# Attention on one core: where two groups of 32-column matmuls stand in the order of rounds

## The chip, the core and the metric

The kernel runs on one core of a Trainium2 chip. The core has a matrix engine (TensorE, PE in the profile, whose weight loads are shown as PEld), VectorE (DVE), ScalarE (ACT), GpSimd (POOL), SyncE (SP), which here only issues DMAs, and 16 DMA engines. All work in parallel, each in the order of its own program, and wait for each other by semaphores. The metric is the device time of one execution in microseconds (us); less is better.

## The reference, cut to what matters

```python
x = x + attention(layernorm(x), ctx, ctx)   # 8 batches, 512 tokens, 512 wide, 16 heads of 32
#   scores = Q K^T / sqrt(32);  attn = softmax(scores);  out = (attn V) Wo^T + bo
h = layernorm(x)
logits = h @ router_weight.T + router_bias  # 8 experts, the best 2 of each token
x = x + sum over the two chosen experts of weight * expert(h)
```

Everything is float32. The experts' part follows the attention and is untouched here.

## The kernel before, in words

The attention is cut into 32 units: 8 batches times 4 groups (c = 0 to 3) of four heads. A unit is worked on in stages that are spread over several steps; a step s is one turn of the pipeline, and `step(s)` writes down, in 8 rounds, what the engines do in it. `ORDER` is the list of all steps' entries, and every engine runs through that one list and picks out its own, so the order within a round is the order on each engine. In what follows c is the remainder of s by 4.

In step s TensorE works on unit s and on three neighbours:

- `max` (row_max, line 443), once in each round: two matmuls of scores of unit s+1 into the one buffer `max_ps`, from which VectorE takes the rows' maxima (line 674, 1024 columns). The `max` of the next round writes the same buffer, so it waits until that reduction has ended (line 431).
- `exp` (line 455), twice in each round: scores again, which ScalarE takes from a work bank through the exponential into `pt` (line 563).
- `weigh` (line 467), in rounds 1, 3, 5 and 7: four heads of `pt` times V. Each matmul has 32 columns of weights, and the four heads fill four strips of 32 columns. Being float32, each matmul appears twice in the trace, so the group of four is 8 records.
- `sum` (line 475), once in a step: the column of ones times `acc`, the sum of the exponentials that GpSimd adds up (lines 754 and 757). It is four matmuls of 32 columns as well. ScalarE copies the result to `inv` (line 569), and VectorE inverts it and divides (`norm`, lines 685 and 690), one quarter in each of four rounds.
- the projections of unit s+2: `k` (line 402, in two halves of 6), `q` (line 410, two halves of two matmuls, 4 records), `v` (line 424, two times 12). Steps with c = 2 have them in other rounds: both halves of `q` in rounds 0 and 1, `k` in rounds 3 and 4. So in a step with c = 2 round 2 holds no projection.
- for finished tokens: the output projection `out` (line 488, two halves of 4 records, in rounds 6 and 7), the transposition `turn_xln` of the normalised rows (line 373, round 5), the router's columns `logits` (route_logits, line 380: four matmuls of 32 columns, one for each quarter of the width), and `logit_sum` (line 386, round 0), which adds the four quarters up.
- `turn_max` (line 449) opens a step: the maxima of unit s are transposed, split by ScalarE (line 553) and VectorE (line 678) and sent by two DMAs to where `exp` of unit s reads them from round 1 on.

The work banks are four buffers of PSUM for everything but `max`, `weigh` and the first tiles. A small planner gives each use, in the order of the list, the bank that has been out of use longest; TensorE then waits until the bank's use before has been read (`take`). Moving an entry therefore also changes which bank, and so which reader, the entries behind it wait for.

In steps with c = 1 ScalarE also normalises the next batch's input in rounds 1 and 2 (`ln1`, line 538). Step 32 and the rounds after it are the end of the attention: the last divisions, output projections, second normalisations and router's columns, one token tile after another.

The lines touched are 151 and 152 (`sum` in round 2), 163 (`logits` in round 6) and 187 (`norm` in rounds 3 to 6).

Of the kernel before, what the change touches and what calls it, by code (L numbers as in the profile page):

```python
# [54 lines left out]
def attention_stage(nc, x, ctx_t, w_t, bq, bk, bv, bo, router_wt, router_b, out, xln_dram, logits, ident):  # L55
    B, S, D = x.shape
    C = D // P
    T = S // P
# [4 lines left out]
    units, bs = range(B * C), range(B)  # L63

    with ExitStack() as ctx:
# [62 lines left out]
        def step(s):  # L128
# [3 lines left out]
            def at(r, *keys):  # L132
                rounds[r] += keys
# [3 lines left out]
            for r in range(8):  # L137
# [10 lines left out]
                    at(r, ("weigh", s - 1, T - 1))  # L148
                if r % 2 and r > 1 and s in units:
                    at(r, ("weigh", s, (r - 3) // 2))  # L150
            if s - 1 in units:
                at(2, ("sum", s - 1))


            if s - 6 in tokens[:-T]:
# [2 lines left out]
            if s - 5 in tokens[:-T]:  # L158
                at(0, ("x2", s - 5))
                at(1, ("rstd", s - 5))  # L160
                at(4 if c == 2 else 3, ("ln2", s - 5))
                at(5, ("turn_xln", s - 5))
                at(6, ("logits", s - 5))
            if s - 4 in tokens[:-T]:
                at(6, ("out", s - 4, 0))
                at(7, ("out", s - 4, 1))
# [17 lines left out]
                        at((r + t) % 8, *keys)  # L184
            if s - 1 in units[:-1]:
                for t in range(T):
                    at(3 + t, ("norm", s - 1, t))

            if s + 2 in units:
                u = s + 2  # L190
# [60 lines left out]

        tokens = range(B * T)
        ORDER = [key for s in range(-2, B * C + 3) for key in step(s)]


# [61 lines left out]
        at = {key: n for n, key in enumerate(ORDER)}  # L317
# [1345 lines left out]
```

## Time and profile before

| | us |
|---|---|
| three runs | 1777.14, 1781.18, 1782.40 |
| median | 1781.18 |
| the profiled execution | 1776.77 |
| its span | 1775.1 |
| TensorE busy in the span | 1633.1 (92%) |
| VectorE busy | 1242.6 (70%) |
| GpSimd busy | 803.3 (45%) |
| ScalarE busy | 654.2 (37%) |

The attention takes the first 998 us of the span, the choice of experts the next 60, the experts the rest. A timeline row gives the start from the span's begin, the duration, the engine, the line, the tiles and how many records were merged into it; what stands in brackets is the idle time of that engine before the row and who ended it. "issue" there means that no wait of a semaphore explains it. A merged row's duration runs from its first start to its last end.

### The profile page before, as it was taken

The page shows a single profiled execution, that of the slowest core. Times are in us where ns is not written, and L with a number is a line of the kernel's source. Part 1 is how long each engine was busy: PE and PEld are TensorE (multiplying, and loading weights), DVE is VectorE, ACT ScalarE, POOL GpSimd, SP SyncE. Part 2 cuts the span into 40 slices and gives each one's busy share as a digit, 9 for nine tenths or more (in the row PEclk, how much of TensorE's full clock was granted, in tenths as well). Part 3 has the DMA queues.
Part 4 walks back from the last instruction along what each step waited for, and adds up shares of the span by engine and source line. Part 5 has one row for each costly group of instructions (what it writes and reads, how often), then busy time and mean ns, then how long its engine had stood idle before and what let it go on. Part 6 is the DMA issues. An engine that isn't in the chain of part 4 may idle for free. (4 is left out here: it accounts for less than half of the span.)

```text
span 1775.1 us, 30007 instructions
## 1 busy us (share of the span) xinstructions
PE 1633.1 (92%) x9637; PEld 1178.9 (66%) x9637; DVE 1242.6 (70%) x2223; ACT 654.2 (37%) x1265; POOL 803.3 (45%) x619
## 2 busy tenths in 40 slices
PE   4798999999999999999997349999999999999996
PEld 3454555555555555555543149999999998999995
DVE  3566667776776777666673668777888778867874
ACT  3253444544445445344442123223333224222321
POOL 3255556555556565555665122333434333343422
PEclk9899999999999999999999559999999999999998
DMA  5332333343433434333321251334443245233422
GB/s 190 96 106 70 98 111 95 95 115 86 124 91 101 109 78 126 86 96 95 95 72 36 69 184 44 90 92 160 147 164 122 89 141 185 94 97 132 126 71 73
DMA packets 98804, 188.69 MB, mean 106 GB/s; under 512 B 26320, under 2 KB 27344, under 8 KB 98640
## 3 DMA queue, kind: packets, MB, share of 16 engines
q1 hardware_dynamic: 79408, 123.99, 24.7%
q0 software_dynamic: 19232, 62.73, 11.1%
q8 instruction: 77, 1.26, 0.3%
q14 instruction: 87, 0.71, 0.1%
HBM read 204.19 MB, written 37.36 MB: 136 GB/s over the span
## 5 line engine op out<-in xcount | busy, mean ns | idle before, releaser
L674 DVE TENSOR_REDUCE negmax<-max_ps 128x2 f32<-128x1024 f32 x256 | 312.4, 1220 | 207.6 <-PE max_ps L443 207.2
L563 ACT ACTIVATE pt<-work 128x512 f32<-128x512 f32 x512 | 278.7, 595 | 274.6 <-PE work L455 261.5
L757 POOL TENSOR_TENSOR acc<-acc,pt 128x1024 f32<-128x1024 f32 x128 | 303.4, 2372 | 134.6 <-ACT pt L563 133.8
L1292 PE MATMUL gu_ps<-xgT_hi,wg_hi 128*128 128x256 f32 x1248 | 355.1, 285 | 0.0
L1292 PE MATMUL gu_ps<-xgT_hi,wg_lo 128*128 128x256 f32 x1248 | 352.0, 282 | 0.0
L1292 PE MATMUL gu_ps<-xgT_lo,wg_hi 128*128 128x256 f32 x1248 | 351.6, 282 | 0.0
L754 POOL TENSOR_TENSOR acc<-pt 128x1024 f32<-128x1024 f32 x64 | 155.6, 2432 | 264.2 <-ACT pt L563 264.2
L1292 PEld LDWEIGHTS gu_ps<-xgT_hi,wg_hi 128*128 128x128 f32 x1248 | 235.7, 189 | 0.0
L1292 PEld LDWEIGHTS gu_ps<-xgT_lo,wg_hi 128*128 128x128 f32 x1248 | 235.7, 189 | 0.0
L1292 PEld LDWEIGHTS gu_ps<-xgT_hi,wg_lo 128*128 128x128 f32 x1248 | 235.5, 189 | 0.0
L443 PE MATMUL max_ps<-ks,qs 96*128 96x512 f32 x512 | 200.6, 473 | 24.3 <-DMA qs<-q_lo 15.4
L1531 POOL DMA_INDIRECT out<-acc,idx x78 | 77.3, 991 | 321.3 <-DVE acc L1440 321.3
L1352 ACT ACTIVATE sig<-gate 128x256 f32<-128x256 f32 x156 | 65.1, 418 | 328.9 <-DVE gate L1404 328.9
L455 PE MATMUL work<-qs,ks 98*128 98x512 f32 x512 | 168.0, 405 | 7.3 <-DMA qs<-m_lo 5.8
L443 PEld LDWEIGHTS max_ps<-ks,qs 96*128 96x128 f32 x512 | 89.5, 193 | 86.7 <-issue 65.0
L467 PE MATMUL o_ps<-pt,v 128*32 128x512 f32 x1024 | 136.4, 605 | 1.3 <-ACT pt L563 1.3
L410 PE MATMUL work<-xT,wq 128*128 128x512 f32 x256 | 126.2, 616 | 5.1 <-ACT pt L563 5.1
L1305 PE MATMUL d_ps<-wd_hi,hid_hi 128*128 128x512 f32 x312 | 124.2, 398 | 5.0 <-DVE acc L1437 5.0
L1526 POOL DMA_INDIRECT acc<-out,idx x78 | 80.5, 1031 | 101.1 <-DMA out<-acc,idx 88.7
L488 PE MATMUL work<-wo,oT 128*128 128x512 f32 x240 | 120.6, 626 | 5.9 <-DVE oT L690 3.4
L455 PEld LDWEIGHTS work<-qs,ks 98*128 98x128 f32 x512 | 95.8, 190 | 43.8 <-issue 12.1
L685 DVE RECIPROCAL inv<-inv 128x128 f32<-128x128 f32 x128 | 120.7, 943 | 4.6 <-ACT inv L569 4.6
(199 smaller groups left out, 2824.6 us busy)
## 6 DMA issues: line engine op xcount, KB each, us to landing
raw_g<-w_gate_up SPq DMA_DIRECT2D x39, 2048.0 KB
raw_d<-w_down SPq DMA_DIRECT2D x39, 1024.0 KB
ks<-k_hi SPq DMA_DIRECT2D x252, 64.0 KB, 2.0
qs<-q_hi SPq DMA_DIRECT2D x252, 64.0 KB, 2.0
bd<-b_down SPq DMA_DIRECT2D x39, 256.0 KB
x_in<-x SPq DMA_DIRECT2D x32, 256.0 KB, 3.1
ctxT_raw<-ctx_t SPq DMA_DIRECT2D x32, 256.0 KB, 4.0
x<-x SPq DMA_DIRECT2D x32, 256.0 KB, 2.9
```

The lines of the kernel that those rows point to most:

```text
L410: ins = e.matmul(to[:, :], wq[:, k, cols], xT[:, k, :], start=(k == 0), stop=(k == C - 1))
L443: ins = e.matmul(max_ps[:, j, :], qs[i][0:3 * HD, h, t * P:(t + 1) * P], ks[i][0:3 * HD, h, :], start=True, stop=True)
L455: e.matmul(to[:, :], ks[i][0:3 * HD + 2, h, k * P:(k + 1) * P], qs[i][0:3 * HD + 2, h, :], start=True, stop=True).then_inc(exp_ready.sem, 1)
L467: ins = e.matmul(o_ps[u % 2][HD * h:HD * (h + 1), :], v[:, k, c * P + HD * h:c * P + HD * (h + 1)], pt[k % 2][:, h, :], start=(k == 0), st ...
L488: ins = e.matmul(to[:, :], oT[b % 2][:, k, t * P:(t + 1) * P], wo[:, k, :], start=(k == 0), stop=(k == C - 1))
L563: e.activation(pt[k % 2][:, h, :], in_work("exp", u, k, h)[:, :], ACT.Exp, scale=scale).then_inc(exped.sem, 1)
L674: e.tensor_reduce(negmax[:, u % 2, n:n + 2], max_ps[:, :, :], AX.X, ALU.max, negate=True).then_inc(maxed.sem, 1)
L685: e.reciprocal(inv[:, cols], inv[:, cols]).then_inc(inverted.sem, 1)
L754: e.tensor_tensor(acc[:, heads, :], pt[0][:, heads, :], pt[1][:, heads, :], ALU.add).then_inc(added.sem, 1)
L757: e.tensor_tensor(acc[:, heads, :], acc[:, heads, :], pt[k % 2][:, heads, :], ALU.add).then_inc(added.sem, 1)
L1292: ins = e.matmul(gu_ps[n % GU_BANKS][:, part, :], wg[s][pw][:, k, cols], xgT[s][px][:, k, :], start=(k == 0 and m == 0), stop=(k == KD - 1 ...
L1305: ins = e.matmul(d_ps[j][:, :], hid[s][px][:, k, j * P:(j + 1) * P], wd[s][pw][:, k, :], start=(k == 0 and m == 0), stop=(k == KF - 1 and ...
```

## The change

`sum` of unit s-1 stands in round 3 instead of round 2, behind that round's `weigh` (in step 32, which has no such `weigh`, it stays in round 2). `logits` of token tile s-5 stands in round 7 instead of round 6, behind that round's `weigh`. The four divisions of a unit stand in rounds 4 to 7 instead of 3 to 6. No instruction is added or removed. The lines behind the change are 2 higher in the changed kernel.

```diff
@@ step(s) @@
                 if r % 2 and r > 1 and s in units:
                     at(r, ("weigh", s, (r - 3) // 2))
-            if s - 1 in units:
-                at(2, ("sum", s - 1))
+
+                if r == (2 if s == B * C else 3) and s - 1 in units:
+                    at(r, ("sum", s - 1))
+                if r == 7 and s - 5 in tokens[:-T]:
+                    at(r, ("logits", s - 5))
...
                 at(5, ("turn_xln", s - 5))
-                at(6, ("logits", s - 5))
...
             if s - 1 in units[:-1]:
                 for t in range(T):
-                    at(3 + t, ("norm", s - 1, t))
+                    at(4 + t, ("norm", s - 1, t))
```

TensorE in step 17 (c = 1), from round 2 to the beginning of round 4; the numbers behind `work` are the banks. Before:

```order
L443 MATMUL max_ps<-ks0,qs0 128x512 x2
L455 MATMUL work1<-qs2,ks2 128x512
L455 MATMUL work3<-qs2,ks2 128x512
L475 MATMUL work2<-acc,ones 32x512 x4
L410 MATMUL work1<-xT,wq 128x512 x2
L443 MATMUL max_ps<-ks0,qs0 128x512 x2
L455 MATMUL work3<-qs2,ks2 128x512
L455 MATMUL work2<-qs2,ks2 128x512
L467 MATMUL o_ps1<-pt0,v 32x512 x4
L410 MATMUL work1<-xT,wq 128x512 x2
L443 MATMUL max_ps<-ks0,qs0 128x512 x2
```

and with the change:

```order
L445 MATMUL max_ps<-ks0,qs0 128x512 x2
L457 MATMUL work1<-qs2,ks2 128x512
L457 MATMUL work3<-qs2,ks2 128x512
L412 MATMUL work0<-xT,wq 128x512 x2
L445 MATMUL max_ps<-ks0,qs0 128x512 x2
L457 MATMUL work1<-qs2,ks2 128x512
L457 MATMUL work3<-qs2,ks2 128x512
L469 MATMUL o_ps1<-pt0,v 32x512 x4
L477 MATMUL work2<-acc,ones 32x512 x4
L412 MATMUL work0<-xT,wq 128x512 x2
L445 MATMUL max_ps<-ks0,qs0 128x512 x2
```

The ones product has moved behind the weighing, and the query projection has bank 0 instead of bank 1, which the first of the two `exp` just ahead of it fills.

TensorE in step 14 (c = 2), rounds 2 and 3. Before:

```order
L443 MATMUL max_ps<-ks0,qs0 128x512 x2
L455 MATMUL work3<-qs2,ks2 128x512
L455 MATMUL work2<-qs2,ks2 128x512
L475 MATMUL work0<-acc,ones 32x512 x4
L443 MATMUL max_ps<-ks0,qs0 128x512 x2
L455 MATMUL work3<-qs2,ks2 128x512
L455 MATMUL work2<-qs2,ks2 128x512
L467 MATMUL o_ps0<-pt0,v 32x512 x4
```

and with the change:

```order
L445 MATMUL max_ps<-ks0,qs0 128x512 x2
L457 MATMUL work1<-qs2,ks2 128x512
L457 MATMUL work0<-qs2,ks2 128x512
L445 MATMUL max_ps<-ks0,qs0 128x512 x2
L457 MATMUL work2<-qs2,ks2 128x512
L457 MATMUL work1<-qs2,ks2 128x512
L469 MATMUL o_ps0<-pt0,v 32x512 x4
L477 MATMUL work0<-acc,ones 32x512 x4
```

Between the `max` of round 2 and that of round 3 only the two `exp` are left.

TensorE in step 11 (c = 3), rounds 6 and 7. Before:

```order
L443 MATMUL max_ps<-ks,qs 128x512 x2
L455 MATMUL work<-qs,ks 128x512 x2
L380 MATMUL work<-xlnT,rw_cols 32x128 x4
L488 MATMUL work<-wo,oT 128x512 x2
L443 MATMUL max_ps<-ks,qs 128x512 x2
L455 MATMUL work<-qs,ks 128x512 x2
L467 MATMUL o_ps<-pt,v 32x512 x4
L488 MATMUL work<-wo,oT 128x512 x2
```

and with the change:

```order
L445 MATMUL max_ps<-ks,qs 128x512 x2
L457 MATMUL work<-qs,ks 128x512 x2
L490 MATMUL work<-wo,oT 128x512 x2
L445 MATMUL max_ps<-ks,qs 128x512 x2
L457 MATMUL work<-qs,ks 128x512 x2
L469 MATMUL o_ps<-pt,v 32x512 x4
L382 MATMUL work<-xlnT,rw_cols 32x128 x4
L490 MATMUL work<-wo,oT 128x512 x2
```

The router's columns now follow the weighing of round 7.

## Rows read from the trace of the kernel before

**Rows 1.** The page: its head, and a row of section 5 (count | busy, mean ns).
```profile
span 1775.1 us, 30007 instructions
...
L685 DVE RECIPROCAL inv<-inv 128x128 f32<-128x128 f32 x128 | 120.7, 943 | 4.6 <-ACT inv L569 4.6
```

**Rows 2.** Windows: busy us of PE, PEld, DVE, ACT, POOL; PEclk, DMA share, GB/s.
```profile
200.00:900.00 700.00, 685.14 (x3475) 381.24 (x3468) 486.60 (x699) 325.06 (x608) 399.62 (x229) 1.00 0.38 100
```

**Rows 3.** Timeline, step 11, rounds 2 to 3: start, us, engine, what [idle before <-releaser].
```profile
376.41 0.63 PE L443 MATMUL max_ps<-ks,qs 96*128 96x512 f32 x2
...
376.88 0.63 PE L455 MATMUL work<-qs,ks 98*128 98x512 f32 x2
...
377.44 1.07 PE L475 MATMUL work<-acc,ones 128*32 128x512 f32 x8
...
378.97 0.19 PEld L410 LDWEIGHTS work<-xT,wq 128*128 128x128 f32 x1 [0.24 <-issue]
379.40 0.19 PEld L410 LDWEIGHTS work<-xT,wq 128*128 128x128 f32 x1 [0.24 <-issue]
...
380.73 0.63 PE L455 MATMUL work<-qs,ks 98*128 98x512 f32 x2
```

**Rows 4.** Timeline, step 11, round 4, which holds no 32-column group.
```profile
384.57 0.63 PE L455 MATMUL work<-qs,ks 98*128 98x512 f32 x2
...
385.16 0.29 PE L424 MATMUL work<-wv_lo,ctxT_hi 128*128 128x256 f32 x1
385.29 0.28 PE L424 MATMUL work<-wv_hi,ctxT_lo 128*128 128x256 f32 x1
...
386.95 0.63 PE L455 MATMUL work<-qs,ks 98*128 98x512 f32 x2
```

**Rows 5.** Timeline, step 11, round 6, with the router's columns.
```profile
390.90 0.63 PE L455 MATMUL work<-qs,ks 98*128 98x512 f32 x2
391.46 0.43 PE L380 MATMUL work<-xlnT,rw_cols 128*32 128x128 f32 x8
...
394.27 0.63 PE L455 MATMUL work<-qs,ks 98*128 98x512 f32 x2
```

**Rows 6.** Timeline, step 14, round 2 and the start of round 3.
```profile
464.33 0.63 PE L455 MATMUL work<-qs,ks 98*128 98x512 f32 x2
464.53 1.22 DVE L674 TENSOR_REDUCE negmax<-max_ps 128x2 f32<-128x1024 f32 x1 [0.29 <-PE max_ps L443]
...
465.89 0.30 PEld L443 LDWEIGHTS max_ps<-ks,qs 96*128 96x128 f32 x2 [0.84 <-DVE negmax L674]
...
466.46 0.84 PE L455 MATMUL work<-qs,ks 98*128 98x512 f32 x2
```

**Rows 7.** Timeline, step 30, round 3 and the start of round 4.
```profile
923.08 1.22 DVE L674 TENSOR_REDUCE negmax<-max_ps 128x2 f32<-128x1024 f32 x1 [0.92 <-PE max_ps L443]
...
924.44 0.30 PEld L443 LDWEIGHTS max_ps<-ks,qs 96*128 96x128 f32 x2 [0.84 <-DVE negmax L674]
```

**Rows 8.** Timeline, step 17, rounds 2 and 3.
```profile
547.78 0.63 PE L455 MATMUL work<-qs,ks 98*128 98x512 f32 x2
...
549.50 1.07 ACT L563 ACTIVATE pt<-work 128x512 f32<-128x512 f32 x2
...
550.13 1.98 PE L410 MATMUL work<-xT,wq 128*128 128x512 f32 x4 [0.73 <-ACT pt L563]
...
552.43 0.63 PE L455 MATMUL work<-qs,ks 98*128 98x512 f32 x2
```

**Rows 9.** Timeline, VectorE at the start of step 15.
```profile
485.24 0.28 DVE L678 TENSOR_TENSOR m_lo<-work,m_hi 16x128 fp32r<-16x128 f32 x1 [1.63 <-ACT m_hi L553]
```

**Rows 10.** Timeline, step 32, end of the attention: router's columns and their copies.
```profile
987.47 0.66 PE L380 MATMUL work<-xlnT,rw_cols 128*32 128x128 f32 x8
...
989.67 0.59 ACT L575 ACTIVATE xlnT<-work 128x512 f32<-128x512 f32 x1
...
991.13 0.28 ACT L581 ACTIVATE parts<-work 128x128 f32<-128x128 f32 x1 [0.88 <-PE work L380]
```

## The prediction

> **What bounds the kernel now.** I began with the page's head [rows 1]: the span is 1775.1 us, and the execution it belongs to took 1776.77. The change touches the attention alone, so the next view was busy time by windows: over 700 us of steady attention TensorE is busy 685.14, VectorE 486.60, GpSimd 399.62, ScalarE 325.06, at full granted clock (1.00 of 2.4 GHz) [rows 2]. There TensorE sets the end, and the question is what TensorE loses between its instructions and where it waits. A busy row can't tell that, since the matmuls' ends are modelled; start-to-start distances can. So I read TensorE's timeline round by round, from the first `exp` of a round to the first `exp` of the next.
>
> A round without a 32-column group shows what full-width work costs: from 384.57 to 386.95 are 2.38 us [rows 4]. Two `exp` and two `max` take 0.47 a pair (376.41 to 376.88 [rows 3]), and 12 `v` matmuls 0.12 each (385.16, 385.29 [rows 4]): 0.94 + 1.44 = 2.38, with nothing lost.
>
> A round with `sum` and half a `q` goes from 376.88 to 380.73, 3.85 us [rows 3]. The `q` half is 4 records at 0.43 (378.97, 379.40 [rows 3]), 1.71; with 0.94 that is 2.65. The `sum` group therefore costs 3.85 - 2.65 = 1.20. Its 8 records run as two waves of four: together 1.07 us, where one takes 0.6, so the second wave starts 0.45 behind the first. Two waves are 0.85 (at 0.43, the pace of a 512-column record) to 0.91 us of streaming, and about 0.32 are lost in going from 128 columns to 32 and back. The round with `logits` and half an `out` goes from 390.90 to 394.27, 3.37 us [rows 5]: the group costs 3.37 - 2.65 = 0.72, though two waves of 128 columns stream for only about 0.25.
>
> The Trainium skill's page "TensorEngine Tiling (Array Packing)", section "Key Properties", says that changing the tiling mode drains TensorE and that changing only the tile does not. The trace agrees as far as it goes: the four heads of one group start without a gap, and each lone group loses about 0.32. Two groups side by side stand nowhere in the trace; by that page the second would cost its streaming alone.
>
> **The change, term by term.** The same instructions run; what changes is neighbours and waits.
>
> 1. `sum` in steps with c = 0, 1 or 3 (steps 1 to 29: 22 of them). In round 2 it costs 1.20 and goes. Behind the weighing of round 3 it adds two waves. Bounds: 0.85 if only streaming is added, 1.20 if every group pays for itself. I take 0.88, the middle of the streaming bounds, because heads within a group change without loss. Gain 0.32 x 22 = 7.0 us. What comes late next in round 2 would be VectorE's reduction, but a round of 2.65 leaves it its 2.13 (term 3).
>
> 2. The bank of `q` in steps with c = 1. There the same round takes 547.78 to 552.43, 4.65 us, 0.80 more than in step 11, and the first `q` waits for ScalarE's exponential, which is late because the normalisation of the input runs ahead of it [rows 8]. With the change `q` takes another bank, long read, and the wait has no cause. The next that needs those exponentials is the `exp` pair of round 3, 2.65 later than 547.78, at 550.4. The wait of `q` ended at 550.13, when the first bank was read; the second is read one exponential on (two take 1.07, so 0.5), 550.6, and the second `exp` wants it at about 550.7. So bounds are 0 and 0.80; I take all 0.80, for 7 steps (1, 5, ... 25; step 29 has no next batch): 5.6 us gain.
>
> 3. `sum` in steps with c = 2 (2, 6, ... 30: 8 steps). Here round 2 is not TensorE's: the reduction starts at 464.53, and the load for the next `max` goes at 465.89, 1.36 later, with VectorE as releaser [rows 6]. In step 30 it is 923.08 and 924.44, again 1.36 [rows 7]. The round takes 464.33 to 466.46, 2.13 us, and `sum` lies inside it for nothing: `max` and `exp` pairs with 1.20 are 2.14, just the time of the reduction's loop. Without `sum` the round stays at 2.13 with TensorE idle in its place, and round 3 grows by 0.88. Loss 8 x 0.88 = 7.0. In step 30 the divisions delay the reduction of round 4 a little, which the shift mends by 0.1 to 0.2; I count 6.9. Bounds: 0 gained in round 2 and 1.20 lost in round 3 at one end, 0.32 gained as in term 1 at the other.
>
> 4. `logits`, 27 token tiles (steps 5 to 31). Round 6 loses 0.72. Behind the weighing two short waves add 0.25 of streaming; but the way back to full width is longer behind a short group: it costs 0.72 against 1.20, 0.48 less, where 0.64 of streaming (8 records of 384 fewer columns in two waves, 0.32 each) is missing, so 0.16 stay. Bounds 0.25 and 0.72; I take 0.40. Gain 0.32 x 27 = 8.6 us.
>
> 5. The divisions one round later. Nothing on TensorE waits for them within three rounds. VectorE's round 7 gets 0.94 for the reciprocal [rows 1], about 0.3 for the product. Behind it stands `m_lo`, for which two DMAs and then `exp` of round 1 wait. Before it VectorE is idle for 1.63 at the fullest place, the end of a step with c = 2 [rows 9]; 1.3 fit, and the step's turn comes 0.4 later by the moved `logits`. Cost 0; if the cover were gone, what sticks out of some 30 steps. ScalarE's copy of the sums and GpSimd's first addition, which waits for `sum`, have a round of slack: 0.
>
> 6. The end. `logits` of tile 27 moves in step 32 from before the transposition of tile 28 to after the last `out`. Before, `logits` of tile 28 started at 987.47 right behind that `out` [rows 10]. Now tile 27 stands there; ScalarE copies tile 28's rows only after it, since both use one buffer; then tile 28 follows. One copy ends at 990.26 and the next one that needs a `logits` after it starts at 991.13 [rows 10], so the way from copy to `logits` and on to a copy is 0.87; with the copy's own 0.59 the detour is 1.46. From there to the end the chain is PE, ACT, PE for each tile, so nothing takes it back. Loss 1.5, bounds 0 and 2. In step 31, where ScalarE sets the pace, the moved `sum` counts 0, between a gain of 0.3 and a loss of 1.2.
>
> Sum: -7.0 - 5.6 + 6.9 - 8.6 + 1.5 = -12.8 us. The profiled execution would take 1764.0. It was 4.4 below the median of 1781.18; I put the change on the median: 1768.4.
>
> **Rivals.**
>
> A. Every group pays for itself, side by side or not (a drain by group, or by the bank it writes). Then terms 1 and 4 are 0, term 3 is 8 x 1.20 less 0.1 = +9.5, and with -5.6 and +1.5 it is 5.4 slower: 1786.6. For it: no pair is in the trace. Against: four heads in four strips follow each other without a gap. By the Trainium skill's rule on tiling modes it would be wrong. It decides when a second group costs over 1.10: at that price terms 1, 3 and 4 (0.10 x 22 gained, 8.7 lost, logits near 0.10 x 27) just eat the rest.
>
> B. VectorE's wait is no loss in steps with c = 2 (as if `sum` had not hidden it): -12.8 - 6.9 - 2.6 = -22, 1759. Two places with the same 1.36 speak against it.
>
> C. The wait of term 2 comes back at round 3, on `exp` or on the weighing: -7.2, 1774. For it: ScalarE is behind by two normalisations. Against: the margin above, thin as it is.
>
> D. `m_lo` comes late through the division in round 7, and `exp` of round 1 waits for its DMA in all steps: 0.4 in each would eat the gain (31 x 0.4 = 12.4), and 0.6 makes it 6 slower, 1787. Against it the idle 1.63.
>
> **How the numbers follow.** Forecast 0.66, A 0.07, B 0.05, C 0.14, D 0.05, something else (the places of the low-clock stretches at start and end) 0.03. The likeliest one's own range is 1763 to 1773: terms 1, 3 and 4 move together with the price of the second group, 0.03 on some 57 groups, 1.7 us; the exit behind `logits` is worth up to 4 to the fast side; the three runs spread by 5.3. With B and C inside, the range is 1759 to 1776. A measurement tells about 0.3%, 5.3 us, from no change. Faster by more holds for the forecast, B and most of C, 0.80; same 0.12; slower 0.08 (A, D).
>
> **What would show it.** In the changed profile: the timeline of step 11 has rounds 2 and 6 at 2.65 and round 3 at 3.84 + 0.88; the round of step 14 stays at 2.13 with the load for `max` still released by VectorE and TensorE idle some 0.9 before it, which is new; step 17 shows no wait on ScalarE at `q`; PE's idle before `m_lo`'s readers is as before. Steps with c = 0 and 3 shorten by 0.64, with c = 1 by 1.44, and those with c = 2 grow by 0.56. If the distance from the weighing's start to that of the ones product is over 0.91, my price is wrong; if round 2 of step 14 gets shorter than 2.13, term 3 is.

## The result, and the profile after

| | before | after |
|---|---|---|
| median, us (lowest to highest) | 1781.18 (1777.14 to 1782.40) | 1761.12 (1759.76 to 1763.00) |
| ratio, with its 95% interval | | 0.9894 (0.9881 to 0.9906) |
| profiled execution, us | 1776.77 | 1761.72 |
| its span | 1775.06 | 1760.01 |

The changed kernel is 1.06% faster by the ratio, 18.9 us at the median before (the medians are 20.1 apart). The forecast was 1768.4 in a range of 1759 to 1776. The profiled pair differs by 15.05 us, against a sum of 12.8; before's profiled execution was 4.4 below its median, after's 0.6 above.

Where sum and traces differ is read from the distances between one `turn_max` and the next, step by step. Us saved by the steps of each kind, as the sum said and as the two traces have it:

| steps | predicted | measured |
|---|---|---|
| c = 0 (4 to 28) | 4.2 | 4.9 |
| c = 1 (1 to 29) | 10.4 | 11.0 |
| c = 2 (2 to 30) | -4.7 | -3.1 |
| c = 3 (3 to 27) | 4.2 | 5.6 |
| step 31 and the end of the attention | -1.2 | -3.0 |
| everything else | 0 | -0.4 |

First the lines of the page and of the windows that answer to [rows 1, 2], with the same columns: count | busy, mean ns | idle; and busy us of PE, PEld, DVE, ACT, POOL, then clock, DMA share, GB/s.

```profile
span 1760.0 us, 30007 instructions
...
L687 DVE RECIPROCAL inv<-inv 128x128 f32<-128x128 f32 x128 | 120.6, 942 | 8.9 <-ACT inv L571 8.9
```

```profile
200.00:900.00 700.00, 684.43 (x3557) 398.37 (x3557) 504.91 (x720) 335.45 (x621) 411.28 (x236) 1.00 0.39 102
```

The same 700 us now hold 82 more matmul records (3557 against 3475, 2.4%), while TensorE's busy time is the same. Steps 8 to 29 together are 2.6% shorter (616.3 us against 632.5). The gain does not show as less idle time, but as more work in the same busy time.

Step 11, rounds 2 to 4, answers to [rows 3]; start, us, engine, what:

```profile
372.86 0.63 PE L457 MATMUL work<-qs,ks 98*128 98x512 f32 x2
...
375.51 0.63 PE L457 MATMUL work<-qs,ks 98*128 98x512 f32 x2
...
376.07 1.06 PE L469 MATMUL o_ps<-pt,v 128*32 128x512 f32 x8
376.95 1.04 PE L477 MATMUL work<-acc,ones 128*32 128x512 f32 x8
...
380.22 0.63 PE L457 MATMUL work<-qs,ks 98*128 98x512 f32 x2
```

Round 2 takes 375.51 - 372.86 = 2.65, round 3 takes 4.71. Round 3 was 3.85, so the ones product behind the weighing costs 0.86, where alone it cost 1.20. From the weighing's start to its own are 0.88.

Rounds 6 and 7 of the same step, to [rows 5]:

```profile
386.54 0.63 PE L457 MATMUL work<-qs,ks 98*128 98x512 f32 x2
...
389.19 0.63 PE L457 MATMUL work<-qs,ks 98*128 98x512 f32 x2
...
389.75 1.07 PE L469 MATMUL o_ps<-pt,v 128*32 128x512 f32 x8
...
390.63 0.40 PE L382 MATMUL work<-xlnT,rw_cols 128*32 128x128 f32 x8
...
390.96 1.98 PE L490 MATMUL work<-wo,oT 128*128 128x512 f32 x4
...
392.78 0.27 PE L451 MATMUL work<-ident,negmax 128*16 128x128 f32 x1
```

Round 6 is 2.65 (it was 3.37). Round 7, up to the next `turn_max`, is 3.60 (it was 3.38): 0.72 go and 0.22 come. From the first record of the router's columns to the `out` behind them are 0.33: two short waves and nothing more.

Step 14, round 2, to [rows 6]:

```profile
457.07 0.63 PE L457 MATMUL work<-qs,ks 98*128 98x512 f32 x2
457.27 1.23 DVE L676 TENSOR_REDUCE negmax<-max_ps 128x2 f32<-128x1024 f32 x1 [0.28 <-PE max_ps L445]
...
458.55 0.30 PEld L445 LDWEIGHTS max_ps<-ks,qs 96*128 96x128 f32 x2 [1.28 <-DVE negmax L676]
458.55 0.73 PE L445 MATMUL max_ps<-ks,qs 96*128 96x512 f32 x2 [0.85 <-DVE negmax L676]
459.12 0.63 PE L457 MATMUL work<-qs,ks 98*128 98x512 f32 x2
```

As forecast, the load still waits for VectorE and TensorE now idles 0.85 where the ones product stood. The round takes 2.05 instead of 2.13: with the ones product gone the load follows the reduction's start by 1.28 instead of 1.36.

Another wait has gone, in round 3. In before the second `exp` of round 3 waited for ScalarE to read the bank:

```profile
466.81 0.19 PEld L455 LDWEIGHTS work<-qs,ks 98*128 98x128 f32 x1 [0.30 <-ACT pt L563]
```

That pair of `exp` took 0.84 from 466.46 on [rows 6]; the same pair in after takes 0.63 from 459.12 on and shows no wait. The banks have changed (see the order of step 14 above): before, round 3 took banks 3 and 2, which the `exp` pair of round 2 had just filled; now it takes 2 and 1.

Step 17, to [rows 8]: the query projection starts 0.47 behind the first `exp` of its round and shows no wait.

```profile
539.58 0.63 PE L457 MATMUL work<-qs,ks 98*128 98x512 f32 x2
...
540.05 1.88 PE L412 MATMUL work<-xT,wq 128*128 128x512 f32 x4
...
542.24 0.63 PE L457 MATMUL work<-qs,ks 98*128 98x512 f32 x2
```

VectorE at the start of step 15, to [rows 9]: the idle time before `m_lo` has fallen from 1.63 to 0.59, and `m_lo` still starts 0.61 behind `turn_max`.

```profile
477.43 0.27 PE L451 MATMUL work<-ident,negmax 128*16 128x128 f32 x1
...
478.04 0.28 DVE L680 TENSOR_TENSOR m_lo<-work,m_hi 16x128 fp32r<-16x128 f32 x1 [0.59 <-ACT m_hi L555]
```

The end, to [rows 10]. Tile 27's router's columns stand at 970.40 and tile 28's wait for the copy between them:

```profile
970.40 0.65 PE L382 MATMUL work<-xlnT,rw_cols 128*32 128x128 f32 x8
971.18 0.60 ACT L577 ACTIVATE xlnT<-work 128x512 f32<-128x512 f32 x1 [8.35 <-PE work L382]
...
971.92 0.66 PE L382 MATMUL work<-xlnT,rw_cols 128*32 128x128 f32 x8 [0.87 <-ACT xlnT L577]
```

One thing that the forecast lacks stands in step 31. Three windows of after, then the one of before at the same place in the program (columns as in [rows 2]):

```profile
895.00:921.00 26.00, 20.74 (x103) 9.68 (x101) 18.62 (x28) 11.73 (x23) 18.59 (x11) 1.00 0.09 31
921.00:928.00 7.00, 6.26 (x22) 2.32 (x26) 1.49 (x1) 3.15 (x6) 3.24 (x4) 0.52 0.21 78
928.00:955.00 27.00, 23.59 (x101) 9.63 (x94) 9.16 (x15) 7.27 (x14) 15.92 (x9) 1.00 0.09 29
```

```profile
941.00:948.00 7.00, 6.52 (x41) 1.91 (x37) 4.91 (x7) 4.77 (x10) 4.50 (x4) 1.00 0.11 40
```

In after's profile the granted clock was 0.52 for 7 us, the lower level of 1.2 GHz, and from the `turn_max` of step 31 to the ones product of step 32 it took 33.38 us against 31.39. Both kernels have the same idle time at its start, here in after's timeline and then in before's:

```profile
921.74 1.19 PE L457 MATMUL work<-qs,ks 98*128 98x512 f32 x2 [2.15 <-DMA qs<-m_lo]
```

```profile
940.23 0.70 PE L455 MATMUL work<-qs,ks 98*128 98x512 f32 x2 [2.15 <-DMA qs<-m_lo]
```

Eleven of the twelve experiments told below show a fall there as well, for 3.4 or 6.8 us, `e4_norm_only` among them, which runs TensorE in the order of before; `e10_low_early` and before show none. Nothing ties the fall to the change. `e10_low_early` runs TensorE in step 31 in after's order, and without a fall it takes 31.09 for the stretch that took 33.38. By that comparison the fall cost 2.3 in after. This stretch is 2.0 of the 3.0 us lost there; the other 1.0 is the tail, from there to the attention's end (30.21 against 29.24).

### The profile page after: what moved, and what is told of

It reads as the page before. It is cut to its first block and busy times, and to the rows that moved or that the text cites. A ratio compares the mean times of both kernels' runs of the same rounds, so it can differ in the third digit from the quotient of the medians.

```text
span 1760.0 us, 30007 instructions
## 1 busy us (share of the span) xinstructions
PE 1615.5 (92%) x9637; PEld 1187.8 (67%) x9637; DVE 1247.7 (71%) x2223; ACT 658.1 (37%) x1265; POOL 800.0 (45%) x619
## 5 line engine op out<-in xcount | busy, mean ns | idle before, releaser
L1307 PE MATMUL d_ps<-wd_lo,hid_hi 128*128 128x512 f32 x312 | 123.6, 396 | 0.0
```

The source lines that it names most:

```text
L1307: ins = e.matmul(d_ps[j][:, :], hid[s][px][:, k, j * P:(j + 1) * P], wd[s][pw][:, k, :], start=(k == 0 and m == 0), stop=(k == KF - 1 and ...
```

## The experiments

Each was timed against runs of the kernel before on the same chip, and the ratio is to those; so two experiments are best compared by their ratios. The lengths of rounds are from the first `exp` of one to that of the next. Means of steps with c = 3 are over steps 11 to 27, those of steps with c = 2 over steps 10 to 26.

**The ones product alone.** The kernel of after with the router's columns back in round 6.

```diff
-                if r == 7 and s - 5 in tokens[:-T]:
-                    at(r, ("logits", s - 5))
...
                 at(5, ("turn_xln", s - 5))
+                at(6, ("logits", s - 5))
```

> Only the ones product moves behind the weighing (round 3) and the divisions one round later; the router's columns stay in round 6. If a second 32-column group pays its streaming alone (0.86 us behind a weighing against 1.20 alone, as the changed kernel's rounds show), 22 steps with c = 0, 1, 3 give 0.34 each (7.5), the wait of the query projection in 7 steps with c = 1 goes (0.65 net each, 4.6), and 8 steps with c = 2 lose 0.56 each (4.5): 7.6 us faster than before, about 1773.5. Rival, all of the gain comes from the sum and its banks: near the changed kernel's 1761. Rival, the sum gives nothing because the steps with c = 2 eat it: within 2 us of before.

1774.17 us, ratio 0.9964 (0.9950 to 0.9978): 6.4 us gained.

**The router's columns alone.** The kernel of before with only `logits` moved to round 7.

> Only the router's columns move behind the weighing of round 7; ones product and divisions as before. Round 6 loses 0.73 and round 7 gains 0.22 in 27 steps: 13.8 us faster, less about 1 for the detour at the attention's end: 12.8 faster than before, about 1768. By the price of the prediction (0.40 behind the weighing, 1.5 at the end) it would be 7.1 faster, 1774.

1774.06 us, ratio 0.9961 (0.9944 to 0.9977): 6.9 us gained, where each of the 27 columns saves 0.50 in its own two rounds, 13.5 in all. Half is missing. Steps with c = 2 did shorten, from a mean of 28.20 to 27.65, but steps with c = 3 grew from 28.25 to 29.17. There the distance from `turn_max` to the first `exp` was 1.3 to 2.5 us in five of six steps (7 to 27), where it is 0.57 when nothing waits, and in steps 15 and 19 the granted clock fell to 0.50 for 3.4 us right behind it. The last runs look for what this wait is.

**The divisions alone.** The kernel of before with `norm` in rounds 4 to 7.

> Only the divisions one round later. Theory: VectorE had the room, 0 within 1 us. Rival, part of the gain comes from reductions of the maxima that start earlier in rounds 4 to 7: 2 to 4 us faster. Rival, the reduced idle time before m_lo costs: slower by 0.3 in each of 31 steps, 9 us.

1780.71 us, ratio 1.0003 (0.9992 to 1.0014): no cost in the time. The trace shows where one is hidden. In steps with c = 1, here 17, `max` behind round 1 now waits for VectorE's reduction, which starts 1.99 behind the first `exp` of the round (0.89 in before):

```profile
546.86 1.21 DVE L674 TENSOR_REDUCE negmax<-max_ps 128x2 f32<-128x1024 f32 x1
...
548.13 0.30 PEld L443 LDWEIGHTS max_ps<-ks,qs 96*128 96x128 f32 x2 [0.46 <-DVE negmax L674]
```

Round 1 of these steps (5 to 25) takes 3.82 to 3.86 instead of 3.54 to 3.59, and round 2, where `q` waits for ScalarE, is shorter by as much (4.32 to 4.38 instead of 4.65).

**Not side by side.** The kernel of after, but the ones product ahead of the two `exp` of round 3, so that it and the weighing are each alone.

```diff
+                if r == (2 if s == B * C else 3) and s - 1 in units:
+                    at(r, ("sum", s - 1))
                 u, j = (s, r - 1) if r else (s - 1, 7)
                 if u in units:
                     at(r, *[("exp", u, j // 2, 2 * (j % 2) + i) for i in range(2)])
```

> The changed kernel with the ones product in the same round 3, but ahead of the two exp instead of right behind the weighing, so that it stands alone among 128-column work; the router's columns still behind the weighing. If neighbourhood is what saves, each of 30 steps loses 0.34 against the changed kernel: 10 us slower than it, about 1771. If what saves is only the other round or the other banks, it is equal to the changed kernel, 1761.

```profile
379.34 1.03 PE L445 MATMUL max_ps<-ks,qs 96*128 96x512 f32 x2
380.30 1.07 PE L477 MATMUL work<-acc,ones 128*32 128x512 f32 x8
381.29 0.73 PE L457 MATMUL work<-qs,ks 98*128 98x512 f32 x2
381.96 1.07 PE L469 MATMUL o_ps<-pt,v 128*32 128x512 f32 x8
```

1771.07 us, ratio 0.9951 (0.9936 to 0.9966). In steps with c = 0 rounds 2 and 3 together take 3.74 + 3.95 = 7.69 us, against 2.65 + 4.71 = 7.36 in after. The same work in the same step costs 0.33 more when the neighbour is full width. That is the price of going to 32 columns and back, measured by itself. Over the 30 steps moved it is 10 us, as expected.

**The bank of `q`.** The kernel of after with one rule in the planner, which gives `q` in steps with c = 1 the bank that the `exp` ahead of it fills, as in before.

```diff
+                if kind == "q" and what[0] % C == 3 and 3 <= what[0] < B * C - C:
+                    bank = free.index(at["exp", what[0] - 2, 0, 2])
```

> The changed kernel, but in the 7 steps with c = 1 in which ScalarE also normalises the next input, the query projection is given the bank of the first exp of round 2 again, as in the kernel before. Theory: round 2 of these steps goes from 2.65 back to about 3.45, with TensorE waiting for ScalarE: 4.6 to 5.6 us slower than the changed kernel, about 1766. Rival, the wait went because the ones product no longer stands between: no difference.

Step 17, round 2 (start, us, what, idle before):

```profile
551.97 0.63 PE L459 MATMUL work<-qs,ks 98*128 98x512 f32 x2
...
554.17 3.15 PE L414 MATMUL work<-xT,wq 128*128 128x512 f32 x4 [1.57 <-ACT pt L567]
```

1778.92 us, ratio 0.9994 (0.9977 to 1.0011): nearly all of the change's gain is gone. The expectation was 1766, and its price for the wait was wrong. Round 2 took 4.45 to 4.49 in four of the seven steps against 2.65, so the wait is 1.84 and not 0.80. In the other three (1, 5 and 17) it took 6.01 to 6.34, because behind the wait the granted clock fell to 0.50 for 3.4 us. In before the bank came free 2.35 us behind the first `exp` of the round [rows 8], and 1.20 of the ones product lay inside that wait; only what stuck out of it, 0.80, showed. The mechanism holds, and it is worth more than its term said: had the planner not given `q` another bank, moving the ones product would have made these steps longer. Round 2 would be 0.2 shorter than in before, and round 3 0.86 longer.

**Steps with c = 2 left as they were.** The kernel of after with the ones product of these steps in round 2.

```diff
-                if r == (2 if s == B * C else 3) and s - 1 in units:
+                if r == (2 if s == B * C or c == 2 else 3) and s - 1 in units:
```

> The changed kernel, but in the steps with c = 2 (2, 6, ... 30) the ones product stays in round 2, where TensorE waits for the reduction anyway. Theory: these 8 steps lose no 0.56 (0.88 by the prediction) any more: 4.5 to 7 us faster than the changed kernel, 1754 to 1757; and if the low-clock stretch in step 31 of the changed kernel comes from the emptier rounds of step 30, about 2 more. Rival, the reduction's wait in round 2 is no free place: equal to the changed kernel or slower.

1758.87 us, ratio 0.9871 (0.9849 to 0.9893), against 1754 to 1757 expected; after's interval overlaps with it, so a gain isn't shown. Rounds 2 and 3 went from 2.05 + 4.37 to 2.13 + 3.73, 0.56 shorter in steps 2 to 26. But again the steps behind them, with c = 3, grew: a mean of 28.20 against 27.51. Part of it is one fall of the clock, to 0.50 for 3.4 us in step 15.

**A shorter reduction.** The kernel of after, in which the reduction of round 2 in steps with c = 2 reads 512 columns instead of 1024. It leaves out half of the scores in that maximum.

> The changed kernel; in round 2 of the steps with c = 2 the reduction looks at half of the columns only (2 times 256 instead of 2 times 512), so the shift of the softmax of those rows is the maximum over half of the keys. Theory: that reduction sets round 2 there. It shrinks from 1.22 to about 0.69, and round 2 from 2.05 to about 1.5: 8 times 0.53, 4 us faster than the changed kernel, 1757. Rival, something else (the work banks, ScalarE's exponentials) holds round 2 there: no difference.

Step 14, rounds 2 and 3:

```profile
458.61 0.69 DVE L677 TENSOR_REDUCE negmax<-max_ps 128x2 f32<-128x512 f32 x1 [0.29 <-PE max_ps L445]
...
459.35 0.30 PEld L445 LDWEIGHTS max_ps<-ks,qs 96*128 96x128 f32 x2 [0.75 <-DVE negmax L677]
...
460.40 0.19 PEld L457 LDWEIGHTS work<-qs,ks 98*128 98x128 f32 x1 [0.52 <-ACT pt L565]
```

1759.54 us, ratio 0.9877 (0.9856 to 0.9899), against 1757 expected; its interval overlaps with after's. Round 2 fell from 2.05 to 1.52, so the reduction does set it. Round 3 grew by the same amount, from 4.37 to 4.89: its second `exp` waits 0.52 for ScalarE. Two limits stand one behind the other there, and the nearer one hid the second.

**The best of these.** The ones product in round 2 in steps with c = 2 and in step 31, and the router's columns of tile 27 back in round 6 of step 32.

> The changed kernel with three parts put back: the ones product in round 2 in steps with c = 2 and in step 31, and the router's columns of tile 27 in round 6 of step 32. Theory: 4.5 from the steps with c = 2, about 1 at the end of the attention, and 0 to 2 in step 31: 6 to 8 us faster than the changed kernel, 1753 to 1755. Rival: no faster than with the steps of c = 2 put back alone.

1757.05 us, ratio 0.9861 (0.9840 to 0.9883), 2 to 4 us short of what was expected; five of six steps with c = 3 had 1.7 to 2.4 us between `turn_max` and `exp` instead of 0.57.

**`k` one round earlier.** Three runs (`e2_logits_only`, `e3_c2_stays`, `e7_best`) now had a shorter step with c = 2 paid back behind it. This one fills TensorE's idle time in round 2 of these steps.

```diff
-                    at(2, ("ctx_lo", b + 1, 2), ("ctx_lo", b + 1, 3))
-                    at(3, ("low", u, "q"), ("k", u, 0))
-                    at(4, ("k", u, 1))
-                    at(5, ("low", u, "k"), ("v", u, 0))
-                    at(6, ("v_out", u, 0), ("v", u, 1))
-                    at(7, ("v_out", u, 1))
+                    at(2, ("ctx_lo", b + 1, 2), ("ctx_lo", b + 1, 3), ("k", u, 0))
+                    at(3, ("low", u, "q"), ("k", u, 1))
+                    at(4, ("low", u, "k"), ("v", u, 0))
+                    at(5, ("v_out", u, 0), ("v", u, 1))
+                    at(6, ("v_out", u, 1))
```

> The changed kernel, but in steps with c = 2 the two halves of k stand in rounds 2 and 3 instead of 3 and 4, the low part of k in round 4 instead of 5, and the two halves of v in rounds 4 and 5 instead of 5 and 6. My theory: round 2 of these steps costs 2.05 us because VectorE's reduction holds it while TensorE is idle, so the first half of k (1.37) fits into it and the round becomes 2.31; round 4 goes from 2.31 to about 2.38, round 6 from 4.08 to 2.65. A step shortens by 0.26 + 0.07 - 1.43 = -1.10, seven steps 7.7 us. The low part of k leaves a round earlier, so the wait for its DMA at the start of the next step with c = 3 (about 0.4 us a step on average in the changed kernel) goes as well: about 2.5 us. Together about 10: 1751 us, ratio to the kernel before near 0.983. Rival (the first k of a new batch is held up by the high and low parts of the context, which ScalarE and VectorE make in rounds 0 to 2): round 2 grows past 3 us and the gain shrinks to 3 us or less. Rival (the 2.05 us are needed by something else than the reduction): round 2 costs its 2.05 plus 1.37, and nothing is gained beyond the DMA wait.

1760.37 us, ratio 0.9886 (0.9860 to 0.9912), where about 1751 was expected: no gain over after, though the steps with c = 2 did what was expected (2.31, 4.41, 2.37, 3.95, 2.65 for rounds 2 to 6; a mean of 27.13 us against 28.39). All of it is given back by c = 3, 28.85 against 27.51. The timeline of the end of step 10 shows who is late. SPq is SyncE issuing DMAs:

```profile
355.56 0.74 DVE L662 SCALAR_TENSOR_TENSOR k_lo<-work,bk_col,k_hi 128x512 fp32r<-128x512 f32 x1
355.62 4.97 SPq L726 DMA_DIRECT2D ks<-k_hi  x8
...
360.63 0.58 SPq L819 DMA_DIRECT2D x_in<-x  x1
...
361.80 3.99 SPq L726 DMA_DIRECT2D ks<-k_lo  x4
...
365.07 0.27 PE L450 MATMUL work<-ident,negmax 128*16 128x128 f32 x1
...
367.41 0.30 PEld L444 LDWEIGHTS max_ps<-ks,qs 96*128 96x128 f32 x2 [2.67 <-issue]
```

VectorE had made `k_lo` by 356.3, but SyncE issues it only from 361.80 to 365.79, because it issues without a pause from 346.23 on: 8 of `q_hi`, 4 of `q_lo`, 8 of `k_hi`, the loads of the next input, a store, about 0.6 us each. After itself has the same row in step 10, from 345.27 to 364.38, with `k_lo` issued from 360.78 to 363.19. `max` of the new step reads `k_lo` and can load 1.62 after the last issue. The trace names no releaser here ("issue"), so the wait is found only by looking at the queue.

Behind that idle time the clock fell too, to 0.59 from 370 to 374:

```profile
364.00:370.00 6.00, 3.58 (x14) 2.14 (x13) 2.93 (x5) 1.35 (x3) 1.84 (x2) 0.99 0.49 141
370.00:374.00 4.00, 4.00 (x16) 2.03 (x14) 2.65 (x5) 1.09 (x2) 3.91 (x4) 0.59 0.18 68
```

**`k_lo` one place earlier in SyncE's queue.** The run `e3_c2_stays` with the low part of `k` at the end of round 4, which on SyncE puts it ahead of the last input load.

```diff
-                    at(4, ("k", u, 1))
-                    at(5, ("low", u, "k"), ("v", u, 0))
+                    at(4, ("k", u, 1), ("low", u, "k"))
+                    at(5, ("v", u, 0))
```

> The changed kernel with the ones product of steps with c = 2 left in round 2 (as in the run e3_c2_stays), and in these steps the low part of k at the end of round 4 instead of in round 5. In e3_c2_stays steps with c = 2 were 0.5 us shorter than in the changed kernel, but steps with c = 3 were 0.7 us longer, in the distance from turn_max to the first exp of round 0, where max waits for the DMA of the low part of k. If that DMA chain is the cause, an earlier start by about a round (1.3 to 2 us) brings this distance back to 0.57 to 0.8 us in every step with c = 3, and the time falls by about 0.8 x 6 = 5 us below e3_c2_stays: about 1753.5 us, ratio near 0.984. Rival (the distance varies with the DMA queue's own load from the start of the step, not with when the low part is made): the distances stay at 0.7 to 2.0 and the time at 1758 to 1760. Rival (the low part, now ahead of VectorE's reduction of round 5, delays it): round 5 to 6 of these steps grows by 0.3 or more.

1755.42 us, ratio 0.9867 (0.9841 to 0.9893). The distances at the start of steps 7 to 19 with c = 3 fell from 1.43 to 2.00 in `e3_c2_stays` to 0.62 to 0.78, and no round of the step grew, so the second and the third answer of the expectation are out. In step 10 the four `k_lo` are now issued from 356.43 on, right behind `k_hi`, with the last load after them: the same DMAs in another order. In time the two runs can't be told apart by their intervals, so the 5 us expected between them are not shown; the mechanism is, in the distances.

**Three loads out of SyncE's full stretch.** The run `e9_k_early` with three of the four input loads moved from the step with c = 2 to the next.

```diff
-                for t in range(T):
-                    at(1 + t, ("load_x", b + 2, t))
+                at(1, ("load_x", b + 2, 0))
                 at(7, ("stats", b + 2, 0))
             if c == 3 and s > 0 and b + 2 in bs:
-                at(1, ("stats", b + 2, 1))
+                for t in range(1, T):
+                    at(2 * t - 2, ("load_x", b + 2, t))
+                at(4, ("stats", b + 2, 1))
```

> The run e9_k_early with one more edit: in steps with c = 2 only one of the four loads of the next input (x_in) is issued, the other three stand in rounds 0, 2 and 4 of the step with c = 3 (the statistics of the second tile move from its round 1 to its round 4). In e9_k_early steps with c = 2 fell to 27.1 us as expected, but steps with c = 3 grew to 28.85, with 1.7 to 2.9 us between turn_max and the first exp instead of 0.57. My theory: SyncE's queue is the cause. In step 10 of that run it issues without a gap from 346.23 to 366.4, some 0.6 us for each DMA: 8 of q_hi, 4 of q_lo, 8 of k_hi, 4 of x_in, one store, 4 of k_lo; the max of round 0 starts 1.6 us after the last k_lo is issued. Three loads fewer ahead of it are 1.74 us: the distances fall to 0.57 to 1.2, steps with c = 3 to about 27.3, and the time by 6 x 1.5 = 9 us to about 1751, ratio near 0.983. Rival (the wait is for the DMA engines or for when VectorE makes the low part, not for the issuing): the distances stay at 1.7 to 2.9 and the time at 1760. Rival (the loads or the statistics are late now, for the normalisation of the input in steps with c = 1): these steps grow by more than 0.5.

The same place as in the run before:

```profile
349.61 4.98 SPq L727 DMA_DIRECT2D ks<-k_hi  x8
350.76 0.74 DVE L663 SCALAR_TENSOR_TENSOR k_lo<-work,bk_col,k_hi 128x512 fp32r<-128x512 f32 x1
...
354.64 0.58 SPq L842 DMA_DIRECT2D xln_dram<-x  x1
355.32 3.59 SPq L727 DMA_DIRECT2D ks<-k_lo  x4
...
360.28 0.27 PE L451 MATMUL work<-ident,negmax 128*16 128x128 f32 x1
360.53 0.30 PEld L445 LDWEIGHTS max_ps<-ks,qs 96*128 96x128 f32 x2 [0.59 <-issue]
```

1751.98 us, ratio 0.9830 (0.9816 to 0.9844), where 1751 and 0.983 were expected. The last `k_lo` is now issued 1.4 us before `turn_max` (it was 0.7 after it), the distances at the start of c = 3 are 0.57 to 0.82, and these steps fell from 28.85 to 27.19. The loads are fewer in SyncE's queue and fewer in the DMA engines there; the run doesn't separate the two. The gap-free queue and the 5.5 us between `k_lo` being made and being issued speak for the queue, and so does `e10_low_early`, which leaves as many loads in the step and changes their order.

**And the ends.** The same with step 31 and tile 27 as in `e7_best`.

> The run e11_loads_later, and as in e7_best the ones product of step 31 in round 2 and the router's columns of tile 27 in round 6 of step 32. If both runs' theories hold, it is 1 to 2 us below e11_loads_later: 1749.5 us, ratio near 0.982. If the end is set by the place of the low-clock stretch in step 31 instead, it is the same within 1 us.

1750.50 us, ratio 0.9815 (0.9802 to 0.9828), the fastest of all; it can't be told from `e11_loads_later`, but both are clearly below after.

## Why the prediction was right, and where its terms were not

The sum had the sign and the main mechanism. Two of its six terms had the wrong size (3 and 4), one (5) left out small costs, one (6) can't be confirmed, and the errors partly cancel, which is luck. The measured 1761.12 lies in the whole range (1759 to 1776) but 2 us below the range that the forecast gave itself (1763 to 1773). The number is as near to rival B's 1759, but B's mechanism did not happen: steps with c = 2 did lose (term 3).

1. The ones product for c = 0, 1, 3. Right: 0.86 where 0.88 was put, 0.34 saved a step. `e5_apart` takes the neighbour away and gives 0.33 back. The Trainium skill's page "TensorEngine Tiling (Array Packing)", section "Key Properties", says that a change of the tiling mode drains TensorE and that a change of the tile does not; `e5_apart` and after agree with it (0.86 beside the weighing, 0.33 more apart from it). Rival A, which had each group pay for itself, is refuted.
2. The bank of `q`. Right in size by the numbers of the trace before (round 2 went from 4.65 to 2.65, which is 1.20 and 0.80), though 0.15 come back in round 1 of the same steps (3.54 to 3.69). `e4_norm_only` shows that these come with the moved divisions, for which VectorE's reduction of round 1 starts late; `e2_logits_only`, with the divisions in place, keeps 3.50 to 3.54 in steps 9 to 29. `e6_bank` shows that the two can't be had apart: without the ones product the old bank would have cost 1.84. Rival C, the wait coming back in round 3, did not happen.
3. Steps with c = 2. The mechanism was right (VectorE releases, TensorE idles 0.85), the size too large: a step loses 0.56 and not 0.88. Round 2 is 2.05 and gives 0.08; by the prediction's own sign, a round under 2.13, the term is off. Round 3 grows by 0.64 only (3.73 to 4.37): the product adds its 0.86, and 0.22 go, because the second `exp` of round 3 no longer waits for ScalarE; by the order of step 14 its bank is another. `e3_c2_stays`, with the product back in round 2, has 3.73 and the wait again. This is the mechanism of term 2; the term priced the moved product and not the banks that move with it.
4. The router's columns. The most mis-sized term: behind the weighing they cost 0.22 and not 0.40, so each saves 0.50 instead of 0.32, 13.5 us instead of 8.6. What failed is the step that read a longer way back to full width out of the lone group (the 0.16): with a 32-column group ahead of it the short group costs its streaming and no more. The lower bound, 0.25, was the right value.
5. The divisions: 0 in the time of `e4_norm_only`, within 2 us, but not nothing in the trace. Besides the 0.15 of term 2, rival D's mechanism shows at the beginning: in steps 2, 3 and 4 `m_lo` starts 1.03, 1.96 and 1.62 behind `turn_max`, against 0.79, 0.70 and 0.61, and `e4_norm_only` has the same late starts while `e2_logits_only` has those of before. In step 4 the first round is longer for it, 3.70 (3.71 in `e4_norm_only`) against 3.09. From step 5 on `m_lo` starts 0.61 behind `turn_max` in both kernels (0.98 in steps with c = 2), and there D is out.
6. The tail. Profiled 0.97 against 1.5 forecast. In the other runs the same stretch takes 27.5 to 31.6 us, depending on where the clock falls, so neither number is confirmed.

With the sizes measured the sum would be about -7.5 - 4.6 + 4.5 - 13.5 + 1.0 = -20. The timed runs give 18.9 to 20.1, the profiled pair 15. Of the missing 5 in the pair, 2.0 are the stretch with the low clock in step 31, which the sum had no term for and which before's profiled execution happened to be spared, and most of the rest is waiting at the start of steps: step 2 has 4.28 for its first round where before has 3.27, step 4 the 0.61 of term 5, step 10 has 0.7 more in its first round, steps 11 and 15 have 0.35 and 0.54 more between `turn_max` and `exp`.

The experiments `e9` to `e11` show the cause of those in steps with c = 3: SyncE issues DMAs without a pause through the step before, and `k_lo` comes late in that queue. Faster steps with c = 2 don't make the queue shorter, so time saved in them is handed back. This was not among the rivals. `e2_logits_only` and `e3_c2_stays` show the same distances grown, and `e10_low_early`, which is the latter with `k_lo` further ahead, takes them away; that this, with the falls of the clock behind it, is also all that `e2_logits_only` misses was not tested. For the first rounds of steps 2 and 10 the cause is open.

## What to carry to other kernels

Put narrow matmul groups next to each other: the change of width costs once for the pair, and the second group costs its streaming alone, however short. Before you price a saving in one step, look at the queue that feeds the next one, with its issues counted and multiplied by the time of one: an engine that issues without a pause is a limit that no busy row shows, and the wait for it can stand as "issue" without a releaser. And a wait may lie over other work: when that work is moved away the whole wait shows, not the part that stuck out. Where a planner hands out buffers in the order of the list, price the buffers that change hands as well as the work that moves.

## What the runs showed of the hardware

- Four float32 matmuls of 128 x 32 weights and 512 columns cost 1.20 us between full-width neighbours and 0.86 behind another such group; with 128 columns 0.72 and 0.22. So the way to 32 columns and back costs 0.34 and 0.50 in these two places, more for the short group, and the second narrow group is spared it.
- One DMA of 64 KB takes SyncE about 0.62 us to issue (8 of `k_hi` in 4.97). The four of `k_lo` took 2.41 in most steps and 3.99 in step 10 of `e9_k_early`, with one slow issue among them; why isn't known.
- The granted clock fell to its lower level behind single idle stretches of TensorE of 1.5 to 2.7 us in the middle of steady work: to 0.59 in `e9_k_early` from 370 us on, to 0.52 in step 31 of after, to 0.50 in steps 1, 5 and 17 of `e6_bank`. The same 2.15 us of idle time in step 31 of before, and the same wait in the other four steps of `e6_bank`, were followed by no fall, so what an idle stretch will cost can't be foretold from its length alone in these traces. A fall cost 1.5 to 2.3 us on top of the wait (rounds 2 of `e6_bank`; step 31 of after against `e10_low_early`).
